# Node work of a four-layer graph network placed inside the stream of neighbour sums

## The reference

```
L0: h = x + sum of x[src] over a node's edges;  relu(relu(h @ W1.T + b1) @ W2.T + b2)
L1: four convolutions: h = relu(sum of norm * (h @ W)[src] + b), the last without relu
    norm = dinv[src] * dinv[dst]; each sum has the node's own row once more
L2: agg = sum of norm * ((x @ Wn + bn)[src] + edge_attr @ We + be);  agg + (h + resid) / degree
L3: two mean convolutions: mean of x[src] @ W_l.T + b_l + x @ W_r.T, relu between them
```

## Time and profile before

| | us |
|---|---|
| median of 3 runs | 2927.76 (2923.49 to 2930.55) |
| profiled execution, its own time | 2929.08 |
| its span in the trace | 2927.4 |
| PE busy | 2622.0 (90%) |
| DVE busy | 1440.5 (49%) |
| ACT busy | 580.7 (20%) |
| POOL busy | 293.4 (10%) |

### The profile page before, as it was taken

One profiled execution on the slowest core, in us unless ns is written; L12 is line 12 of the kernel. 1 busy time (PEld: TensorE's weight loads), 2 busy tenths in 40 slices (PEclk: granted clock), 3 DMA queues, 4 the chain that ended last, 5 costly groups with the idle time before them and its releaser, 6 DMA issues.

```text
span 2927.4 us, 41999 instructions
## 1 busy us (share of the span) xinstructions
PE 2622.0 (90%) x16407; PEld 1489.4 (51%) x16407; DVE 1440.5 (49%) x5009; ACT 580.7 (20%) x554; POOL 293.4 (10%) x151
## 2 busy tenths in 40 slices
PE   0699999949999899989998999949998699989996
PEld 0467666625545455555555555544445444464445
DVE  5999999786667534363335434482002500050005
ACT  1588999610001100020002000020000100010000
POOL 3300000000000111311110211125000000020000
PEclk9699999979999999999999999969999799999998
DMA  7249444539996798868985988609995499949993
GB/s 204 78 174 158 184 185 177 223 113 369 365 365 237 240 310 307 279 218 305 305 300 192 311 305 304 216 29 308 302 303 175 167 302 302 305 142 305 303 303 108
DMA packets 241118, 715.77 MB, mean 245 GB/s; under 512 B 48635, under 2 KB 63695, under 8 KB 237337
## 3 DMA queue, kind: packets, MB, share of 16 engines
q1 hardware_dynamic: 213196, 644.87, 66.8%
q10 hardware_dynamic: 26924, 66.25, 6.4%
q0 software_dynamic: 800, 1.94, 0.2%
HBM read 621.04 MB, written 91.96 MB: 244 GB/s over the span
## 4 chain that ended last, share of the span: by engine, by line
PE 70%; DVE 20%; DMA 3%; DVEq 3%; issue 2%; ACT 1%; POOL 0%; SPq 0%; ACTq 0%; POOLq 0%
PE PS L1285 67%; DVE S L776 7%; DVE S L775 7%; PE PS L1405 2%; DMA HR<-adjacency 1%; DVE XN L872 1%; DMA XN<-in_x_dram 1%; PE PS L1508 1%; DVEq L900 1%; DVE ST L854 1%; DVE HN L898 1%; DVE HN L891 1%; DVE MV L860 0%; DMA TB<-adjacency 0%; DVEq L943 0%
## 5 line engine op out<-in xcount | busy, mean ns | idle before, releaser
L1285 PE MATMUL PS<-HR,AGN 128*128 128x500 f16 (+1 forms) x6580 | 1349.1, 355 | 51.9 <-DVE AGN L665 36.1
L1285 PEld LDWEIGHTS PS<-HR,AGN 128*128 128x128 f16 x6580 | 631.2, 97 | 661.8 <-issue 65.8
L1285 PE MATMUL PS<-S,AGN 128*128 128x500 f16 (+1 forms) x2156 | 470.6, 368 | 0.7 <-DMA S<-adjacency 0.6
L776 DVE TENSOR_SCALAR S<-S,RBW 128x245 f16<-128x245 f16 x1250 | 428.8, 477 | 0.0
L775 DVE TENSOR_SCALAR S<-iot,RBW 128x128 f16<-128x128 f16 x1250 | 421.2, 451 | 1.6 <-PE PS L1285 1.4
L1285 PE MATMUL PS<-S 128*128 128x245 f16 x1250 | 336.6, 276 | 30.3 <-DVE S L776 27.4
L1285 PE MATMUL PS<-TB,AGN 128*128 128x500 f16 (+1 forms) x1750 | 330.7, 323 | 11.0 <-DMA TB<-adjacency 10.9
L1285 PEld LDWEIGHTS PS<-S,AGN 128*128 128x128 f16 x2156 | 205.5, 96 | 232.5 <-DMA S<-adjacency 1.5
L628 POOL TENSOR_TENSOR TB<-TB,dstI 128x1088 f32<-128x1088 f32 x49 | 146.3, 2985 | 1588.6 <-DVE mxe L1009 1588.6
L960 DVE SCALAR_TENSOR_TENSOR AT<-PS,SC,RBW 128x500 f32<-128x500 f32 (+1 forms) x65 | 46.7, 719 | 505.2 <-PE PS L1285 501.5
L1013 DVE TENSOR_SCALAR mce<-PS 128x1 f32<-128x1 f32 x49 | 7.8, 158 | 475.6 <-PE PS L1419 475.6
(11 more groups left out here) (176 smaller groups left out, 1851.7 us busy)
## 6 DMA issues: line engine op xcount, KB each, us to landing
HR<-adjacency SPq DMA_DIRECT2D x378, 875.0 KB, 5.6
S<-adjacency SPq DMA_DIRECT2D x147, 875.0 KB, 5.5
TB<-adjacency SPq DMA_DIRECT2D x63, 875.0 KB, 4.9
adjacency<-HN SPq DMA_DIRECT2D x9, 3062.5 KB, 10.6
TB<-source_lanes ACTq DMA_DIRECT2D x49, 544.0 KB, 7.1
TB<-in_edge_attr_dram ACTq DMA_DIRECT2D x48, 544.0 KB, 4.6
adjacency<-HR SPq DMA_DIRECT2D x8, 3062.5 KB, 9.9
adjacency<-TB SPq DMA_DIRECT2D x8, 3062.5 KB, 9.9
```

The lines of the kernel that those rows point to most:

```text
L776: v.tensor_scalar(HOT[:, h + P:h + P + HC], iotC, CT[:, t:t + 1], None, ALU.is_equal).then_inc(s_oh, 1)
L1285: return t_.matmul(out_, w, m, start=start, stop=True, skip_group_check=True)
```

## The change

Passes 1 to 7 become one stream of 637 pieces (`ALL`), numbered n, with 8 further steps behind (`TAIL`). Each engine has one loop over n, and the node work of a unit stands in it at a fixed lag, in pieces, behind the unit's last piece (tables `LAG`, `SOON`, and `DUE` made from them). A unit's node work covers the 3 or 4 whole blocks of 128 nodes that its sums complete (`BE`); columns left over go into the next unit's part of `AT`.

- The halves have two buffers, in `AGN` and in `HN`; a pass reads one and writes the other (`HL`). The first unit of a pass waits for the halves that each piece needs (`NEED`), not for all of them.
- Scales come from bounds: the lengths of the weights' columns and the largest bias (`lengths`, `bounds`), for passes 3 and 4 also from the largest value of the rows one pass earlier (`bound_next`). Nothing waits for the largest value of the rows that are to be split.
- Sums use three PSUM banks instead of up to seven; the others hold the node work.
- The edge groups lie in passes 2 and 3 instead of 2, 3 and 4. The edge sums are loaded into `RB` in pass 4 at its piece 28, instead of ahead of pass 5.
- Pass 0's node work runs chunk by chunk: normalising and the high half are now on ACT, with the low half two chunks behind on DVE.
- POOL's work for layer 2 moves to DVE (`second`). The factors `1/count` of passes 6 and 7 are applied after the product instead of before it.
- The result is stored unit by unit from ACT's queue, instead of chunk by chunk from SP's.

```diff
+        LAG = {"hidden": {1: 2}, "rows": {1: 4, 2: 2, 3: 2, 4: 1, 5: 1, 6: 1, 7: 1}, "norm": {4: 2, 5: 2, 7: 2},
+               "turn": {4: 4, 5: 4, 6: 3}, "second": {4: 5}, "low": {1: 5, 2: 3, 3: 3, 4: 6, 5: 3, 6: 2}}
...
+        EP = [PCS + 8 + g * (2 * PCS - 12) // (NG - 1) for g in range(NG)]
+        LP = [1 + g * (PCS - 6) // (NG - 1) for g in range(NG)]
...
@@ SyncE
+                for n in range(ALL):
+                    p, i = n // PCS + 1, n % PCS
...
+                    if p == 4 and i == 4 * PIECES:
+                        sp.wait_ge(s_at, ats(3, NU - 1))
                         for k in range(2):
                             sp.wait_ge(s_ew[k], 16 * len(range(k, NG, 2)))
                         sp.dma_start(RB, Wd[:, MARGIN:MARGIN + NP]).then_inc(s_ewl, 16)
...
@@ GpSimd
+                bias_1()
+                pool.wait_ge(s_ns, 1)
                 for g in range(NG):
-                    if g == GR[3][0]:
-                        residual_bias(1, 1)
                     weighted(g)
-                neighbour_rows()
-                residual_2()
-                residual_bias(5, 7)
+                bias_5()
...
@@ VectorE
+            for q in range(NQ + 2):
+                if q < NQ:
+                    rows_0(q)
+                if 0 < q <= NQ:
+                    factors_0(q - 1)
+                if q > 1:
+                    low_0(q - 2)
...
+                for n in range(ALL + TAIL):
+                    p, i = n // PCS + 1, n % PCS
+                    if p <= LASTP and i % PIECES == PIECES - 1:
+                        sums(p, i // PIECES)
+                    for step in ("low", "rows", "norm", "second"):
+                        for p_, u in DUE[step].get(n, ()):
+                            STEPS[step](p_, u)
...
+                    if n in LOOK_AT:
+                        degrees(LOOK_AT[n])
...
+                    if n in EDGES_AT:
+                        g = EDGES_AT[n]
+                        if g + 1 < NG:
+                            scale(g + 1)
+                            hots(g + 1)
+                            lows(g + 1)
+                        add(g)
...
@@ TensorE
+                if j == 0 and idx(p, u) >= 3:
+                    pe.wait_ge(s_at, NS_ + idx(p, u) - 2)
...
+                if u == 0:
+                    pe.wait_ge(s_split, NQ + j + 1 if p == 1 else splits(p - 1, NEED[j] - 1))
+                pe.wait_ge(s_al[m], 16 * (slot_turns(m) * (p - 1) + i // RING + 1))
...
+                for n in range(ALL + TAIL):
+                    if n < ALL:
+                        piece(n)
...
+                    for step in STEPS:
+                        for p_, u in DUE[step].get(n, ()):
...
+                            STEPS[step](p_, u)
```

More of the change, by code:

```diff
@@ new lines, in due @@
+        def due(step):
+            at_ = {}
+            for p, lag in LAG[step].items():
+                for u in range(NU):
+                    late = SOON.get(step, {}).get(p, lag) if u == NU - 2 else lag
+                    at_.setdefault(PCS * (p - 1) + PIECES * u + PIECES - 1 + late, []).append((p, u))
+            return at_
+        DUE = {step: due(step) for step in LAG}
+        NEED = [next(k + 1 for k in range(NU) if BE[k] >= min(QB * (j + 1), NB)) for j in range(PIECES)]
+        EP = [PCS + 8 + g * (2 * PCS - 12) // (NG - 1) for g in range(NG)]
@@ L327, in own @@
             return out_
[L329 to L344, removed]
+        w_ = 2 * SD_ * QB
+        SLOTS = [HR[:, :].bitcast(f16)[:, k * w_:(k + 1) * w_] for k in range(RING - 1)] + [S5[:, :].bitcast(f16)]
         end = slice((NG - 1) * J, NT)
@@ new lines, in neighbours @@
+            def neighbours(p, u):
+                b0, b1 = blocks(u)
+                n = b1 - b0
+                t = temp(6, u)
+                dve.wait_ge(s_y, idx(6, u) + 1)
+                v.tensor_copy(t, Y2[:, 0:n * P])
+                dve.drain()
+                for b in range(n):
+                    c_ = slice(b * P, (b + 1) * P)
+                    last = v.scalar_tensor_tensor(out=t[:, c_], in0=Y[:, c_], scalar=rc[:, b0 + b:b0 + b + 1], in1=t[:, c_],
+                                                  op0=ALU.mult, op1=ALU.add)
+                last.then_inc(s_yfree, 1)
+                dve.drain()
+                v.tensor_tensor(three(t), three(t), bias(4, n), ALU.add)
+                dve.drain()
+                v.tensor_scalar(t, t, 0.0, None, ALU.max).then_inc(s_t, 1)
@@ new lines, in high, with store @@
+            def high(p, u):
+                if u == 0 and p in (1, 2, 3):
+                    act.wait_ge(s_scale, p + 1)
+                if p == 5:
+                    act.wait_ge(s_xn, normed(p, u))
+                else:
+                    act.wait_ge(s_t, made(p, u))
+                c.activation(HI[(p + 1) % 2][:, node_cols(u)], XN[:, node_cols(u)] if p == 5 else temp(p, u), ACT.Copy,
+                             scale=SC[:, p + 1, 0:1]).then_inc(s_hi, 1)
+            def store(u):
+                b0, b1 = blocks(u)
+                act.wait_ge(s_xn, normed(7, u))
+                if u == NU - 1:
+                    act.dma_start(out[(NB - 1) * P:N, :], blk(XN)[0:NTAIL, NB - 1, :]).then_inc(s_out, 16)
+                    b1 -= 1
+                act.dma_start(rows(out[b0 * P:b1 * P, :]), blk(XN)[:, b0:b1, :]).then_inc(s_out, 16)
@@ L1316, in sub_pass @@
                 a3 = A16[s % 3].rearrange("p (h c) -> p h c", h=NB)
[L1317 to L1318 removed]
+                for part in (HI[0], LO[0]):
+                    last = mm(AG2[s % 2], part[:, k * P:(k + 1) * P], a3[:, k, :], start=first and part is HI[0])
                 return last
@@ new lines, in edge_scale, with edge_group @@
+            def edge_scale(g):
+                pe.wait_ge(s_aem, g + 1)
+                if g:
+                    pe.wait_ge(s_sce, g)
+                t_.matmul(SM, ones[:, :], mxe[:, g % 2:g % 2 + 1], start=True, stop=True).then_inc(s_esm, 1)
+            def edge_group(g):
+                pe.wait_ge(s_ahl, g + 1)
+                if g:
+                    pe.wait_ge(s_eae, g + 1)
+                for j in range(J):
+                    last = mm(CH[:, 0:WIN], AHL[g % 2][:, j, :], OHW[g % 2][:, j, :], start=j == 0)
+                last.then_inc(s_eam, 1)
```

1334 lines of the change are left out of this document (723 added, 611 removed).

## The result

| | before | after |
|---|---|---|
| median, us (fastest to slowest) | 2929.16 (2923.49 to 2932.26, 4 runs) | 2764.55 (2762.81 to 2766.54, 4 runs) |
| ratio to before | | 0.944, interval 0.9424 to 0.9457 |
| span of the profiled execution, us | 2927.4 | 2761.8 |
| first lookup on TensorE, us | 640.74 | 646.40 |
| end of the last sum, us | 2877.0 | 2751.9 |

The account below looks back on a forecast made before the run. PE bounds the stream, a chain of PE, DVE and ACT the windows (281.5 us). 632 + 282 + 1654 + 144 + 12 + 19 = 2743 in the span, median 2744; range for 8 in 10: 2716 to 2830.

Parts of the forecast that it names:

- the start: Pass 0 up to the first lookup on PE: at 632 us, between 623 and 640, against 640.74 before; 9 us gained.
- the stream: Passes 1 to 7 without windows: 282 us for pass 1, 1654 for passes 2 to 7, 144 for node products.
- the tail: From the last sum to the end of the kernel: 12 us instead of 50.4.
- the rival of products at double cost: Windows hidden, but f32 products among f16 pieces cost double: 144 us more, 2888; chance 4%.
- The port conflict: Start of pass 1: POOL's bias additions to XN delay DVE's lookups; 0 to 16 us for PE, 5 taken.
- the edge sums: Middle of pass 4: PE waits beside the 3.2 MB load into RB, 0 to 10.9 us, 4 taken.
- everything else: Remaining added waits, such as products waiting for a unit's sums, scale wait, a new ACT function's table: 6 us.
- The first unit of pass 5: Pass 4's last low half takes some 3.2 us against a 2.96 us piece before the next pass needs it: 1 us.
- edge groups: Closer together in their passes, PE waits for DVE's halves up to 1 us a time in four places; 3 us taken.
- the 19 of the forecast: All waits that the change adds, together: 19 us, from 3 to 60.
- PE waits for DVE: Rival: each of 98 meetings at lookups and edge groups costs 1 us, giving 2824, or 2873 at 1.5 us; chance 16%.
- The round trip: Rival: DVE answers late for each of 91 units; 2.2 us a unit uses up the gain, 3 us gives 2998; 4%.

Follow-up runs that it names:

- the relu three ahead: In the kernel with all three, the relu of chunk q+3 of pass 0 was put ahead of root and halves of chunk q on ACT: 2737.19 us, ratio 0.935.
- the kernel with all three: Changed kernel with first lookup behind piece 9, POOL's additions spread behind edge groups, and relu of chunk q+2 ahead of root of chunk q: 2744.22 us, ratio 0.938.

## Why the prediction was right, and where it was 20 us off

In spans, 2761.8 against 2743: the start took 14.4 more, the stream with its waits 6.5 more, the tail 2 less.

- **The stream, right.** Windows gone, node products at PE's price: eight f32 products among pieces of pass 7's last unit took 2742.67 - 2740.88 = 1.79, the rate of the earlier trace rows, so the rival of products at double cost (2888) fell. (The prediction reads pass 1 as 283 us and adds 282; that is 1 us.) From the first lookup to the last sum it took 2751.9 - 646.4 = 2105.5, against 282 + 1654 + 144 + 19 = 2099. A pass of edge groups stayed under 330 us.
- **The start, mis-sized, and the main part of the miss.** The step was 7 chunks at 7.2 us of DVE, then ACT's last chunk, tables and lanes: 632. DVE's own chunk took 6.7, so less than forecast; but I had put the waits among the chunks at nothing, and they were 7.7 us (1.45 + 3.25 + 3.03, for rows from PE). The loop over the chunks is a ring of PE, ACT and DVE, and ACT's order, not DVE's work, set its pace; the relu three ahead shows it. What follows, ACT's last chunk, the index tables and the first lane transfer, had 7 us in the sum and took 16.4: 6.6 of waits for ACT (3.35 + 3.25), then 9.75 from the last low half to the first lookup. In these lie POOL's additions: the three tables took 6.2 us in place of 1.4, and the two masks 4.95 where one alone takes 0.79. DVE's chunks began 0.9 earlier than the 574.8 of the sum and took 1.8 less than forecast, so 7.7 + 9.4 - 2.7 = 14.4, and the first lookup came at 646.40, beyond the 640 of the range for this term.
- **What I did not ask about the start:** what stands behind the waiting lookup. Four pieces were ready or nearly so in PE's row. That the wait could be filled by a number in a table was worth some 20 us, more than all new waits together.
- **The port conflict, right in kind, wrong in place.** 5 us were put on lookups in pass 1. Lookups waited 3.3 us, with the additions there or elsewhere, so not for them; the conflict cost some 7 us at the index tables, which have no slack. Each table step took about as long as one addition (2 us), and 14.27 us of additions made 3.26 us of masks 16.55. The Trainium skill, "SBUF — State Buffer", section "SBUF: two separate sides", says that the shared ports are locked for a whole instruction where the DVE operation reads two SBUF inputs or runs in its two-port mode; these traces agree. The prediction has these additions in pass 3 before; the trace before has them at 1232.46, at the end of pass 2.
- **Waits for transfers, mis-sized.** I had 4 for the edge sums and 6 for everything else. The piece behind the edge sums' load waited 1.72, the starts of the passes 9.7 and the short units 0.8, a wait that the prediction does not name: the windows of before had time to refill the ring. The run with the short unit's sums made twice shows that the short pieces are its cause. One more wait, 2.10 in pass 3, has another cause, which is open. The first unit of pass 5 took 0.29 (forecast 1), edge groups 1.2 (forecast 3). That all waits behind the start came to 19.1, the 19 of the forecast, is by chance.
- **The rest of 6.5 us** is mostly cold clock, which the prediction had left out with the windows: 2.3 us in the piece behind the first lookup, 1.4 at pass 2's start and 1.7 behind the wait of 2.10 in pass 3. Some 1 us is not accounted for.
- **The tail, right:** 0.66, six products, and the end 9.9 us behind the last sum; forecast 12.
- **PE waits for DVE (2824), wrong:** DVE is busy 197 of 316 us, 62% where 65% were forecast, and PE's waits for it behind the start are 5.5 us. **The round trip (2998), wrong:** its price was measured, 1.1 us a unit without lag, half of the 2.2 from which it would have decided.
- Of the signs set down beforehand, DVE's share, the tail and the length of passes came, and so did a granted clock of 0.99 to 1.00 over each pass, though not in every slice from 630 on; the first lookup near 632, the last piece near 2731 (2751.9), no gap over 3 us (one of 3.70), and under 25 us of waits for DVE (28.7 with the first lookup) did not.

What stays open: with the lookups later and closer together PE waits 6.4 us for them in place of 3.3. Whether that can be spared, or the loads at the starts of passes be hidden without a larger ring, was not tried, and no run separates the parts of the change other than the scales and the lag.

## What to carry to other kernels

When work is moved into a stream, look at what the idle windows had been paying for: here they refilled a ring of four loads. And look at what stood beside another engine's work: before, POOL's additions ran at the end of pass 2 where DVE had 11.8 us to spare, and PE waited for nothing there. Before counting a wait at the start of a stream as fixed, read what stands in order behind the waiting instruction; ready work behind it is the cheapest gain. And a ring of engines over chunks is paced by the order within its rows: write down each row's waits, not only its work.

## What the runs showed of the hardware that was not expected

- Many DVE operations from SBUF to SBUF lost nearly the whole time of POOL's additions of 128 x 896 f32, not a part of it: 17 masks took 3.26 us alone and 16.55 beside 14.27 us of additions, a copy of 49 columns 0.18 and 2.05, a shift of 833 integers 0.59 and 1.75. Not all did: in the run with later lookups, beside the additions, reading a unit's sums out of PSUM took 0.85 for two (0.86 without additions), and a reduction of 128 columns with one SBUF input 0.27 (0.28 without).
- A short wait can cost PE more than itself, but does not always. Behind waits of 3.3 to 4.3 us at pass 2's start 28 matmuls took 7.44 to 7.76 us in six kernels; behind 3.63 with later lookups and 3.77 with the relu three ahead they took 6.08, at a granted clock of 1.00. No run shows what decides it.
- 16-bit sums of 250 columns use up loads faster than a ring of four refills: 1.5 us a piece against 4.1 us from issue to landing for the small loads and 5.3 for the large ones behind them. With 3 us a piece, the waits at starts of passes fell from 8.6 us in the kernel with all three to 0.3.
